# A graph layer on one core: one tile's rows picked by TensorE in 23 of 24 groups in place of 21

## The chip, the cores and the metric

One NeuronCore of a Trainium2 chip runs the kernel. The metric is device time in microseconds (us) of one execution. In the profile TensorE is PE (PEld its weight loads), VectorE DVE, ScalarE ACT, GpSimd POOL and SyncE SP.

## The reference

One layer of a graph network over 12,500 nodes with 64 features and 400,000 edges, sorted by destination, with 16 features each:

```python
m_in = concatenate([x[src], x[dst], edge_attr], axis=-1)
h = silu(m_in @ W1 + b1)
messages = silu(h @ W2 + b2)
agg = segment_sum(messages, dst, num_segments=12500)
node = silu(concatenate([x, agg], axis=-1) @ W3 + b3)
out = layernorm(x + node)
```

What matters here is `x[src]`: for every edge one row of `x` has to be fetched, in no order.

## The kernel before

**Tiles and groups.** Edges are taken in groups of 1024, as T = 8 tiles of 128 edges. There are 390 full groups and a short one of five tiles. Each tile is 128 rows of `edge_in`: a one-hot of the destination inside a window of 48 nodes (`OH`), the 64 features of the source node (`XS`) and the 16 of the edge (`EA`). `edge_in` has S = 12 slots, one a group. A body is B = 24 groups; there are 16 bodies and a rest. Every engine's order is written out by hand, as `step(g)` for g = 0 to 389.

**Gathers.** GpSimd issues one indirect DMA for each tile (`gather`, L508), eight to a group, with one index for each partition. From group 12 on, `refill` waits until TensorE has transposed the group that held the slot (`s_in_T`).

**Picks.** For some groups (`PICK_OF`) the last tile's rows (`PICKED` = 7) aren't gathered but picked by TensorE out of a copy of `x` that stays in SBUF (`parts`: two parts whose sum is x, 98 blocks of 128 nodes). GpSimd then issues seven gathers. A pick has two rounds (`ROUNDS`), as a PSUM bank holds 8 blocks of 64 features and there are 16 `PLACES`. It has NP = 13 pieces, seven in round 0 and six in round 1. A piece is two matmuls (`pick_piece`, L1086), one for each part, with the one-hot `rows_T` as weights and 512 columns moving; piece 6 holds two blocks only and moves 128 columns. So a pick is 24 matmuls of 512 and two of 128 columns. Three banks (`PICK_BANKS`) take the rounds in turn: the first piece of round number `at` waits until VectorE has read round `at - 3` (`s_picked`).

VectorE's part of a pick: `make_diag` (L827) and `make_rows` (L833, L836) build the keys and `rows_T` three and two groups ahead of the pick's first piece, with `find_rows` (L814 to L820) once for a chunk of eight groups; `pick` reads round 0 (L848), then round 1 (L852), and sums into `edge_in` (L854). TensorE spreads the keys in between (`spread_keys`, L1060).

**Which piece goes where.** `spot(piece)` gives the group in whose step TensorE runs a piece. `read_in` gives the group in whose step VectorE reads a round: the group of the round's last piece, or the one before when that piece is among the first `HALF_STEP` of its step.

```python
def spot(piece):
    return FIRST + piece * B // (PER_BODY * NP)
while spot(ended(PICKS, ROUNDS - 1)) + LEAD + 1 < FULL:
    PICKS += 1
TARGET = [spot(ended(n, ROUNDS - 1)) + LEAD + 1 for n in range(PICKS)]
HALF_STEP = PER_BODY * NP // (2 * B)
def read_in(n, r):
    e = ended(n, r)
    return spot(e) - (e < HALF_STEP or spot(e - HALF_STEP) < spot(e))
```

**TensorE's step(g)**: first layer of group g+1 (L1044, L1045); transposes of group g+2 (L1027), which wait for its gathers, its one-hots, and its picked rows if it has any; the pieces of g (L1086); a wait for the messages of g (`s_pair`, L801); second layer of g+1 (L1050), which waits for `h_T`; the key matmul, half of a lot's update (L1102) in two groups of a body, and the sums of group g (L1069).

**VectorE's step(g)**: bias of g+1 (L779, waits for L1050), window added (L807), one-hots of g+4 (L761 to L765), messages of g+1 paired (L790 to L801), `make_rows`, `make_diag`, `pick`, then a share of a lot.

**ScalarE's step(g)**: first silu of g+1 (L588), copy of the transposed g+2 (L584), edge features of g+4 (L579), second silu of g+1 (L592). In bodies 1 to 15 a lot of nodes that are complete is finished beside the groups: VectorE takes the mean in group 12 of the body, the squares in 13 and the variance in 14 (L884, L886). Behind the work of that step ScalarE waits for the variance, takes the root (L607) and loads the silu table again (L608), before it goes on with the first silu that TensorE's step of group 15 needs.

**SP** loads chunks of eight groups, and for each group a window of destination terms behind `s_z1`, and loads and stores the lots.

Of the kernel before, what the change touches and what calls it, by code (L numbers as in the profile page):

```python
# [23 lines left out]
def gnn_layer(nc, x, src, dst, edge_attr, W1, b1, W2, b2, W3, b3, out):  # L24
# [51 lines left out]

    PER_BODY = 21
    PICKED = T - 1  # L80
    PARTS = 2
    ROW_SETS, HOTS = 3, 4
# [15 lines left out]
    def spot(piece):  # L98
        return FIRST + piece * B // (PER_BODY * NP)

# [15 lines left out]
    KEYS_IN, ROWS_IN, DIAG_IN = ({b - back: n for n, b in enumerate(BEGUN)} for back in (2, 2, 3))  # L116
    HALF_STEP = PER_BODY * NP // (2 * B)

# [1075 lines left out]
```

## Time and profile before

| | |
|---|---|
| median of 3 runs | 3527.44 us (3524.67 to 3528.28) |
| the profiled execution | 3528.14 us |
| its span, first to last instruction | 3526.2 us |
| PE busy | 3265.4 us (93%), 18748 matmuls |
| PEld busy | 2500.9 us (71%) |
| DVE busy | 2965.4 us (84%) |
| ACT busy | 1052.2 us (30%) |
| POOL busy | 2642.7 us (75%), 2791 gathers |
| mean granted TensorE clock | 0.989 of full speed |

An engine's busy time is the union of its instructions' durations. Matmuls overlap, so the duration of one is longer than the time from its start to the next one's. Idle time is put down to what released the engine, "issue" where the profile shows nothing. All rows come from one profiled execution, whose start is 0.

### The profile page before, as it was taken

The page shows a single profiled execution, that of the slowest core. Times are in us where ns is not written, and L with a number is a line of the kernel's source. Part 1 is how long each engine was busy: PE and PEld are TensorE (multiplying, and loading weights), DVE is VectorE, ACT ScalarE, POOL GpSimd, SP SyncE. Part 2 cuts the span into 40 slices and gives each one's busy share as a digit, 9 for nine tenths or more (in the row PEclk, how much of TensorE's full clock was granted, in tenths as well). Part 3 has the DMA queues.
Part 4 walks back from the last instruction along what each step waited for, and adds up shares of the span by engine and source line. Part 5 has one row for each costly group of instructions (what it writes and reads, how often), then busy time and mean ns, then how long its engine had stood idle before and what let it go on. Part 6 is the DMA issues. An engine that isn't in the chain of part 4 may idle for free. (4 is left out here: it accounts for less than half of the span.)

```text
span 3526.2 us, 55961 instructions
## 1 busy us (share of the span) xinstructions
PE 3265.4 (93%) x18748; PEld 2500.9 (71%) x18748; DVE 2965.4 (84%) x6391; ACT 1052.2 (30%) x1687; POOL 2642.7 (75%) x2801
## 2 busy tenths in 40 slices
PE   4899999999999999999999999999999999999996
PEld 2677777777777777777777777777777777777774
DVE  7788888888888888888888888888888888888886
ACT  1322323323333233322323232232322323223232
POOL 7777777777777777777777777777777777777774
PEclk9899999999999999999999999999999999999998
DMA  7112221211222122122211212112121211222111
GB/s 176 36 36 42 40 42 35 49 36 37 40 42 42 36 45 39 37 40 42 42 35 38 46 35 42 36 38 46 38 40 36 49 35 38 40 42 42 34 31 28
DMA packets 324212, 150.08 MB, mean 43 GB/s; under 512 B 213310, under 2 KB 278879, under 8 KB 323926
## 3 DMA queue, kind: packets, MB, share of 16 engines
q0 software_dynamic: 89312, 91.63, 13.8%
q1 hardware_dynamic: 232774, 54.48, 7.4%
q8 instruction: 156, 2.56, 0.3%
q14 instruction: 130, 1.06, 0.1%
q10 hardware_dynamic: 1840, 0.34, 0.1%
HBM read 136.61 MB, written 9.62 MB: 41 GB/s over the span
## 5 line engine op out<-in xcount | busy, mean ns | idle before, releaser
L508 POOL DMA_INDIRECT edge_in<-in_x_dram,src_i x2791 | 2641.6, 946 | 852.1 <-issue 819.9
L1086 PE MATMUL pick_ps<-parts,rows_T 128*128 128x512 f32 (+1 forms) x8684 | 2052.7, 389 | 30.9 <-DVE kept L848 17.1
L1086 PEld LDWEIGHTS pick_ps<-parts,rows_T 128*128 128x128 f32 x8684 | 1554.4, 188 | 386.4 <-DVE kept L848 24.7
L592 ACT ACTIVATE z_ps<-z_ps,zero_col 128x512 f32<-128x512 f32 x391 | 258.8, 662 | 2107.1 <-DVE z_ps L779 2107.1
L1027 PEld LDWEIGHTS in_ps<-ident,edge_in 128*128 128x128 f32 x3128 | 339.4, 142 | 461.2 <-issue 314.6
L779 DVE TENSOR_TENSOR z_ps<-z_ps,b_rep 128x512 f32<-128x512 f32 x391 | 273.3, 699 | 395.7 <-PE z_ps L1050 395.1
L1027 PE MATMUL in_ps<-ident,edge_in 128*128 128x128 f32 x3128 | 427.5, 280 | 130.7 <-DMA edge_in<-in_x_dram,src_i 94.8
L1050 PEld LDWEIGHTS z_ps<-w_bd,h_T 128*128 128x128 f32 x3128 | 411.0, 194 | 70.1 <-issue 32.4
L584 ACT COPY in_T<-in_ps 128x1024 f32<-128x1024 f32 x391 | 396.9, 1015 | 194.1 <-PE in_ps L1027 189.5
L1050 PE MATMUL z_ps<-w_bd,h_T 128*128 128x128 f32 x3128 | 423.5, 279 | 33.7 <-ACT h_T L588 26.3
L1044 PE MATMUL z_ps<-in_T,w_in 128*64 128x512 f32 x782 | 411.8, 608 | 1.3 <-ACT in_T L584 1.2
L1045 PE MATMUL z_ps<-in_T,w_in 128*64 128x512 f32 x782 | 411.8, 608 | 0.0
L854 DVE TENSOR_REDUCE edge_in<-kept 128x64 f32<-128x512 f32 x334 | 355.5, 1064 | 11.5
L836 DVE TENSOR_TENSOR rows_T<-agg_ps,key_of 128x896 fp32r<-128x896 f32 x334 | 361.4, 1082 | 0.0
L794 DVE TENSOR_TENSOR z_ps<-z_ps,beyond 128x512 f32<-128x512 f32 x391 | 273.5, 699 | 13.5
L798 DVE TENSOR_REDUCE pair<-z_ps 128x64 f32<-128x512 f32 x391 | 270.3, 691 | 13.4
L588 ACT ACTIVATE h_T<-z_ps,b_col 128x512 f32<-128x512 f32 x391 | 266.5, 682 | 20.9 <-PE z_ps L1045 20.9
L790 DVE TENSOR_REDUCE every<-z_ps 128x64 f32<-128x512 f32 x391 | 266.0, 680 | 1.7 <-ACT z_ps L592 1.7
L852 DVE COPY_PREDICATED kept<-hot_place,pick_ps 128x512 f32<-128x512 int32 x334 | 244.1, 731 | 12.9
L848 DVE TENSOR_TENSOR kept<-pick_ps,hot_place 128x512 f32<-128x512 f32 x334 | 229.3, 687 | 15.2 <-DVE edge_in L854 0.5
L765 DVE TENSOR_TENSOR edge_in<-agg_ps,dst_rel 128x384 f32<-128x384 f32 x391 | 215.1, 550 | 0.0
L1069 PE MATMUL agg_ps<-edge_in,pair 128*64 128x48 f32 x1564 | 127.1, 242 | 4.0 <-DVE pair L801 4.0
(104 smaller groups left out, 1468.5 us busy)
## 6 DMA issues: line engine op xcount, KB each, us to landing
edge_in<-in_x_dram,src_i POOLq DMA_INDIRECT x2791
ea<-in_edge_attr_dram SPq DMA_DIRECT2D x48, 512.0 KB, 4.5
w_in<-node_terms SPq DMA_DIRECT2D x391, 12.0 KB
node_terms<-h_T SPq DMA_DIRECT2D x12, 256.0 KB, 2.4
node_terms<-lot_T SPq DMA_DIRECT2D x12, 256.0 KB, 2.4
y<-in_x_dram SPq DMA_DIRECT2D x15, 192.0 KB, 5.1
term<-node_terms SPq DMA_DIRECT2D x15, 192.0 KB, 5.0
out_dram<-y SPq DMA_DIRECT2D x15, 192.0 KB
```

The costliest lines, as they stand in the source:

```text
L508: pool.indirect_dma_start(out=edge_in[:, to_slot, t, XS], out_offset=None, in_=x[:, :], in_offset=bass.IndirectOffsetOnAxis(ap=indices[:, ...
L584: nc.scalar.copy(in_T[:, :, :], in_ps[:, :, :]).then_inc(s_in_c, 1)
L779: nc.vector.tensor_add(z2, z2, b2_rep[:, :].unsqueeze(1).to_broadcast([P, T, H])).then_inc(s_biased, 1)
L794: nc.vector.tensor_mul(messages, messages, beyond[:, v % 4, :].rearrange("p (a c) -> p c a", a=2).unsqueeze(3).to_broadcast([P, HT, 2, H]) ...
L798: nc.vector.tensor_reduce(pair[:, v % 2, 1, :], z2_ps[:, :].rearrange("p (k f) -> p f k", f=H), AX.X, ALU.add).then_inc(s_other, 1)
L836: nc.vector.tensor_tensor(rows_T[:, n % ROW_SETS, :, :], agg_ps[:, KEYS].unsqueeze(1).to_broadcast([P, SETS, P]), key_of[:, :].unsqueeze(2 ...
L854: nc.vector.tensor_reduce(edge_in[:, TARGET[n] % S, PICKED, XS], kept[:, :, :].rearrange("p k f -> p f k"), AX.X, ALU.add).then_inc(s_row, 1)
L1027: last = nc.tensor.transpose(in_ps[:, t // HT, t % HT * P:(t % HT + 1) * P], edge_in[:, s, t, :], ident[:, :])
L1044: nc.tensor.matmul(z1_ps[0:H, :], w_in[:, v % NW, :], in_T[:, 0, :], start=True, stop=True)
L1045: nc.tensor.matmul(z1_ps[H:P, :], w_in[:, v % NW, :], in_T[:, 1, :], start=True, stop=True).then_inc(s_z1, 1)
L1050: last = nc.tensor.matmul(z2_ps[:, c * P:(c + 1) * P], h_T[:, c * P:(c + 1) * P], w2_bd[:, :], start=True, stop=True)
L1086: last = nc.tensor.matmul(pick_ps[at % PICK_BANKS][:, 0:(b - a) * H], rows_T[:, n % ROW_SETS, c, :], parts[:, j, a:b, :].rearrange("p k f ...
```

## The change

One constant. In a body, 23 groups have their last tile picked in place of 21. Everything that is worked out from `PER_BODY` follows: how many picks there are (`PICKS`), where each piece stands (`spot`), which groups are picked (`TARGET`), when keys and rows are made, and when rounds are read (`HALF_STEP` goes from 5 to 6).

```diff
-    PER_BODY = 21
+    PER_BODY = 23
     PICKED = T - 1
     PARTS = 2
     ROW_SETS, HOTS = 3, 4
```

## Rows read from the trace of the kernel before

**Rows 1.** The chain that ended last, shares of the span by line.
```profile
POOL edge_in L508 17%; PE pick_ps L1086 4%; DMA edge_in<-in_x_dram,src_i 3%; PE in_ps L1027 2%; PE z_ps L1050 1%; PE z_ps L1044 0%; PE agg_ps L1102 0%; DVE z_ps L779 0%; PE agg_ps L1069 0%; PE pick_ps L1102 0%; DVE edge_in L765 0%; DVE beyond L764 0%; DVE sums L807 0%; DVE z_ps L794 0%; DVE every L790 0%
```

**Rows 2.** Groups of the whole span: shapes xcount | busy, mean ns | idle before, releasers.
```profile
L508 POOL DMA_INDIRECT edge_in<-in_x_dram,src_i x2791 | 2641.6, 946 | 852.1 <-issue 819.9 <-PE in_ps L1027 30.2 <-DMA src_i<-in_src_dram 2.0
L1086 PE MATMUL pick_ps<-parts,rows_T 128*128 128x512 f32 x8016 | 2034.3, 401 | 30.9 <-DVE kept L848 17.1 <-DVE kept L852 12.7
L1086 PEld LDWEIGHTS pick_ps<-parts,rows_T 128*128 128x128 f32 x8684 | 1554.4, 188 | 386.4 <-DVE kept L848 24.7 <-DVE rows_T L836 23.0 <-issue 15.2
...
L836 DVE TENSOR_TENSOR rows_T<-agg_ps,key_of 128x896 fp32r<-128x896 f32 x334 | 361.4, 1082 | 0.0
L854 DVE TENSOR_REDUCE edge_in<-kept 128x64 f32<-128x512 f32 x334 | 355.5, 1064 | 11.5
...
L852 DVE COPY_PREDICATED kept<-hot_place,pick_ps 128x512 f32<-128x512 int32 x334 | 244.1, 731 | 12.9
L848 DVE TENSOR_TENSOR kept<-pick_ps,hot_place 128x512 f32<-128x512 f32 x334 | 229.3, 687 | 15.2 <-DVE edge_in L854 0.5
...
L827 DVE TENSOR_SCALAR key_diag<-ident,find 128x128 fp32r<-128x128 f32 x334 | 96.3, 288 | 1.7
```

**Rows 3.** Who waited for whom, whole span: us in total, times, longest.
```profile
PE in_ps L1027 <- DMA edge_in<-in_x_dram,src_i: 94.8, 126, 4.1
```

**Rows 4.** Stretches: length, busy PE, PEld, DVE, ACT, POOL (instructions), PEclk, DMA share, GB/s.
```profile
120.80:423.30 302.50, 298.05 (x1732) 229.67 (x1733) 262.88 (x569) 90.42 (x146) 228.51 (x243) 1.00 0.21 40
423.30:631.00 207.70, 201.77 (x1159) 155.32 (x1161) 179.20 (x389) 63.59 (x102) 157.07 (x167) 0.98 0.21 40
837.40:1043.50 206.10, 199.49 (x1159) 153.28 (x1159) 179.35 (x389) 63.50 (x102) 155.84 (x166) 1.00 0.21 40
1886.70:2100.50 213.80, 200.25 (x1161) 153.25 (x1161) 179.64 (x389) 63.71 (x102) 161.71 (x172) 1.00 0.20 40
423.30:513.20 89.90, 85.44 (x478) 65.32 (x478) 74.54 (x162) 27.80 (x44) 68.05 (x72) 0.96 0.22 42
3470.50:3499.70 29.20, 18.44 (x102) 12.91 (x101) 16.93 (x36) 9.68 (x14) 19.07 (x21) 0.77 0.13 24
```

**Rows 5.** Timeline of PE, steps 7 and 11: start, us, what, count.
```profile
156.23 5.36 PE L1086 MATMUL pick_ps<-parts,rows_T 128*128 128x512 f32 x22
161.43 1.05 PE L1050 MATMUL z_ps<-w_bd,h_T 128*128 128x128 f32 x8
...
189.41 5.57 PE L1086 MATMUL pick_ps<-parts,rows_T 128*128 128x512 f32 x24
194.82 1.05 PE L1050 MATMUL z_ps<-w_bd,h_T 128*128 128x128 f32 x8
```

**Rows 6.** Timeline of PE and DVE, steps 4 and 8, around bank waits.
```profile
129.26 0.61 PE L1044 MATMUL z_ps<-in_T,w_in 128*64 128x512 f32 x1
...
131.08 3.67 PE L1086 MATMUL pick_ps<-parts,rows_T 128*128 128x512 f32 x16
...
134.55 0.68 DVE L848 TENSOR_TENSOR kept<-pick_ps,hot_place 128x512 f32<-128x512 f32 x1
...
135.29 1.65 PE L1086 MATMUL pick_ps<-parts,rows_T 128*128 128x512 f32 x6 [0.53 <-DVE kept L848]
...
162.63 0.61 PE L1044 MATMUL z_ps<-in_T,w_in 128*64 128x512 f32 x1
...
168.59 2.10 PE L1086 MATMUL pick_ps<-parts,rows_T 128*128 128x512 f32 x8 [0.42 <-DVE kept L852]
```

**Rows 7.** Timeline of DVE and PE, around group 15 of body 1.
```profile
431.16 0.17 DVE L886 TENSOR_SCALAR var<-var 128x6 f32<-128x6 f32 x1
...
433.90 2.04 PE L1050 MATMUL z_ps<-w_bd,h_T 128*128 128x128 f32 x8 [3.37 <-ACT h_T L588]
```

**Rows 8.** Timeline of PE, the last steps.
```profile
3494.69 0.67 PE L1044 MATMUL z_ps<-in_T,w_in 128*64 128x512 f32 x1
...
3499.68 0.61 PE L1044 MATMUL z_ps<-in_T,w_in 128*64 128x512 f32 x1
```

## The prediction, made before the change was built

> **What bounds the kernel now.** I read the chain that ended last first: the largest share it names is GpSimd's issue of gathers [rows 1]. The list of groups says why: 2791 gathers of 946 ns leave GpSimd idle for 852.1 us, of which 819.9 us is issue and 30.2 us a wait for TensorE [rows 2]. So it is always issuing, one gather each (2641.6 + 852.1) / 2791 = 1.25 us. TensorE waits 94.8 us for their landing [rows 3].
>
> The table of stretches then shows that this holds for only part of the run [rows 4]. A body is 24 groups and repeats itself. The stretch from the step of group 39 to that of group 63 (423.3 to 631.0 us) takes 207.7 us, the one two bodies later starting at 837.4 takes 206.1, while 171 gathers need 171 x 1.25 = 213.8 us: GpSimd, which began 12 groups ahead, is being caught up, and TensorE sets the pace, with 199.5 busy of 206.1 us. Five bodies on, one takes 213.8 us, GpSimd's pace. I take 206.3 for TensorE's own pace (near the lower of the two, as 207.7 holds a stretch of half clock), so it has only some 7.5 us to spare in a body, 0.3 us a group. This slack, not the 93% of the page, is what the change spends.
>
> **Gathers removed.** PICKS goes from 334 to 366 (the loop that sets it, counted), so 32 gathers go: a body has 23 x 7 + 8 = 169, or 211.3 us, and the whole floor of GpSimd falls by 40 us. That helps only where GpSimd is the bound.
>
> **Matmuls added.** Each pick is 26 matmuls, 24 of 512 columns and two of 128. The step of group 7 holds 22 long ones and no short: from 156.23 to the L1050 at 161.43 us, 0.236 us each. That of group 11, 22 long and two short, goes from 189.41 to 194.82 us, 5.41 against 5.20, so the short pair is 0.2 us [rows 5]. A pick costs 24 x 0.236 + 0.20 = 5.9 us, and two more in a body 11.8 us, its key matmul hidden in the rounding. They stand in TensorE's order ahead of the second layer, and nothing covers them once the 7.5 us are used: 206.3 + 11.8 = 218.1 us, already above 211.3. Bounds: the weight load alone, 0.188 us, below; 2034.3 / 8016 = 0.254 us, the busy time by count, above [rows 2]; 9.4 to 12.6 us a body. The 401 ns of one overlap and are no price. Even 9.4 leaves 215.7, above 211.3.
>
> By LDWEIGHTS the same bodies look far less full: 153.3 of 206.1 us, 74% [rows 4]. The Trainium skill, Perfetto Trace Analysis, Identifying the Most-Contended Engine, calls matmul busy time a bad measure of the distance to roofline and puts LDWEIGHTS busy % in its place. By that rule a quarter of TensorE would be free and the 12 us would fit: it is the first rival below. I go by the pace, since 24 groups took 206 us while GpSimd's gathers were ahead.
>
> **The wait for banks.** There are three PSUM banks, so a round waits until VectorE has read the round three before. I place each wait by hand. Pick k of a body begins 13k/24 pieces into its step (before: 1.625k), so offsets now creep: 0 0 1 1 2 2 3 3 ... 11, where they jumped 0 1 3 4 6 8 9. VectorE reads a bank at a fixed point: in the step that starts at 129.26 its L848 runs 134.55 to 135.23 and TensorE resumes at 135.29, 6.0 us into the step [rows 6]. At offset 1 TensorE has seven long pieces of 0.47 us and a short one of 0.2 behind its start at 131.08, and stands there 5.3 us into the step; each piece of offset moves that by 0.47 us. That is a wait of 1.2 us at offset 0, 0.7 at 1, 0.25 at 2, none from 3. For picks 1 to 5 of a body: 1.2 + 0.7 + 0.7 + 0.25 + 1.05 = 3.9 us (pick 5 meets find_rows, 0.8 us ahead of the reads in that VectorE step). The first round of a pick waits too, for the second round of two picks before, once that one is read a group later (from pick 12 on): in the step at 162.63 TensorE reached offset 8 and lost 0.6 us until L852 was done [rows 6]. Now five picks (14 to 18) meet this, at offsets 7, 8, 8, 9, 9, each with some 0.2 of key_diag's 288 ns ahead of the read: 1.3 + 0.8 + 0.8 + 0.3 + 0.3 = 3.5 us. Sum 7.4 us, against 3 x (0.74 + 0.6) = 4.1 us now: +3.3 us a body. Bounds: nothing, and twice this.
>
> **The wait for ScalarE at group 15 of a body.** ScalarE holds the next silu back until the lot's variance is there, then loads a table. In TensorE's pace: variance (L886) at 431.16, L1050 at 433.90 after 3.37 us idle [rows 7]. Today that VectorE step holds only L848 ahead of the variance. With offsets of the new rule both reads and the L854 sum stand there: + 0.16 + 0.77 + 1.0 = 1.9 us. Against it VectorE is less late from the steps before, whose TensorE steps are a piece longer (two of them with lot work, each 0.47 us longer: about 1 us less late, an estimate), and the matmuls ahead of the wait end 0.47 us later: net +0.5 us. Bounds 0 and +2. A half clock followed such waits: 0.96 in the 89.9 us from 423.3, 1.00 in the body from 837.4 [rows 4]; its cost is inside the 206.3.
>
> **VectorE and the rest.** 32 picks more are 32 x (1082 + 1064 + 731 + 687 + 288 ns) = 123 us of VectorE [rows 2]. In a body it was busy 179.4 of 206.1 us [rows 4]; with 7.7 us more in 221.9 it has more air, and I price it at nothing beyond the waits above. ScalarE issues nothing new. SP's chunks, windows and lots are unchanged in number and wait for L1045, so they slide with TensorE; no DMA is added. GpSimd will wait for TensorE to free slots, which costs nothing.
>
> **Sum.** A body: 206.3 + 11.8 + 3.3 + 0.5 = 221.9 us, TensorE's pace all through. The step of group 3 starts at 120.8 us, that of group 39 302.5 us later [rows 4]; these 1.5 bodies gain 1.5 x 15.1 = 22.6, so 445.9. Fourteen bodies: +3106.6 = 3552.5 (group 375). The last ten groups with pieces took 89.9 us in TensorE's pace [rows 4]; with 10/24 of 11.8, 1.2 of bank waits and 0.5: 96.5, so 3649.0. Four steps with no pieces, 3499.68 - 3494.69 = 5.0 us each [rows 8], give 3669; now they wait for gathers and take 29.2 us [rows 4]. The last 26.5 us (3499.7 to the end at 3526.2) stay. Span 3695.5; around it lie 1.9 us (3528.1 against 3526.2), so 3697 us. The profiled execution is 0.7 us above the median of the runs, less than I can price.
>
> **Rivals.** (1) The other sign: GpSimd stays the bound, because TensorE's 26% without weight loads is usable; the time is 3528 - 40 = 3488 us. The point that decides is a TensorE body below 211.3 us, where the measured one plus bare matmuls is 218.1. (It is what the page of the Trainium skill named above would have.) For it: TensorE's largest wait is for gathers [rows 3]. Against: rows 4. 4%.
> (2) The waits do not grow: a body of 217.9 to 218.1, hence 1.5 x 3.3 + 14 x 3.8 + 1.7 = 60 us less, 3637 us. The later bodies show waits that vanish when TensorE starts late. But in TensorE's pace nothing makes it late. 10%.
> (3) The waits compound: the wait at group 15 grows by 2 us and each is followed by the half clock, as at 423.3 (207.7 against 206.1, another 1.6 us, of which 0.2 is in my 206.3). Each of 15 bodies costs up to 3 us more and some 2.5 in the mean: 3735 us. 12%.
> (4) Gathers and matmuls trade evenly: 211.3 against 211 or so, about 3527. It needs matmuls at half price. 2%.
> That the change does not do what it says I rule out by the count of PICKS.
>
> **Numbers.** My forecast has 72%, rivals 2 and 3 are its flanks, so the range runs 3630 to 3740. A measurement here tells 0.2% (7 us) from no change. Faster: rival 1, 4%. Within 0.2%: 2%. Slower: 94%.
>
> **What would show it.** Matmuls at L1086 9516, gathers 2759. GpSimd's wait for L1027 hundreds of us instead of 30.2; TensorE's wait for gathers near nothing. Bodies near 222 us from the second on. L1086's idle time before it grown from 30.9 us [rows 2] to some 80 to 110; L1050's wait for h_T near 4 us in every body. Wrong would be bodies at 211 us, or a GpSimd that still never waits, or waits at offsets other than those listed.

## The result, and the profile after

The changed kernel takes **3722.94 us** (median of four runs, 3720.05 to 3725.03), against 3527.86 us (3524.67 to 3530.31, four runs) for the kernel before. The ratio is 1.0552, 95% interval 1.0538 to 1.0565: slower by 5.5%, 195 us. Forecast was 3697 us in a range of 3630 to 3740.

The page of the changed kernel, its span and its busy times:

```profile
span 3723.2 us, 58073 instructions
PE 3482.3 (94%) x19612; PEld 2671.5 (72%) x19612; DVE 3088.6 (83%) x6615; ACT 1052.4 (28%) x1687; POOL 2611.4 (70%) x2769
```

TensorE is busy 217 us longer than the 3265.4 before, at nearly the same share; VectorE 3088.6 - 2965.4 = 123.2 us longer. GpSimd is busy 31 us less, and that helps nobody: the chain that ended last, which began with 17% of gathers [rows 1], now holds no line of GpSimd, though it is short and reaches back only to 3585.8 us, so the groups and stretches below have to carry the reading. The groups of the whole span, shapes and count, then busy time and mean ns, then idle time before them and its releasers:

```profile
L508 POOL DMA_INDIRECT edge_in<-in_x_dram,src_i x2759 | 2610.2, 946 | 991.7 <-issue 852.5 <-PE in_ps L1027 137.2 <-DMA src_i<-in_src_dram 2.0
L1086 PE MATMUL pick_ps<-parts,rows_T 128*128 128x512 f32 x8784 | 2228.4, 401 | 94.0 <-DVE kept L848 47.7 <-DVE kept L852 45.2
L1027 PE MATMUL in_ps<-ident,edge_in 128*128 128x128 f32 x3128 | 436.2, 283 | 11.4 <-DVE edge_in L765 11.4
L1050 PE MATMUL z_ps<-w_bd,h_T 128*128 128x128 f32 x3128 | 429.6, 282 | 73.6 <-ACT h_T L588 57.6 <-DVE pair L801 16.0
```

Against [rows 2]: 32 gathers fewer, and 768 long matmuls more. The transposes (L1027) wait no more for a gather, where they lost 94.8 us [rows 3]; GpSimd waits for the transposes instead, 137.2 us against 30.2. The idle time before the pick matmuls went from 30.9 to 94.0 us, and VectorE's two reads of banks (L848, L852) share it. Each group says where to look next: who is late has changed from GpSimd to TensorE.

The table of stretches, in the columns of [rows 4]: the steps of groups 3 to 37, then a body each in the second, fourth and tenth place.

```profile
120.80:439.50 318.70, 309.14 (x1767) 238.64 (x1769) 268.89 (x575) 88.04 (x142) 240.94 (x256) 1.00 0.17 37
447.40:671.60 224.20, 214.51 (x1213) 164.76 (x1211) 186.93 (x403) 63.65 (x102) 169.65 (x180) 0.98 0.18 39
895.90:1119.20 223.30, 213.38 (x1212) 163.85 (x1211) 187.02 (x402) 63.69 (x102) 163.95 (x174) 0.99 0.18 38
2237.90:2460.80 222.90, 213.33 (x1210) 164.21 (x1209) 186.61 (x402) 63.70 (x102) 159.14 (x169) 0.99 0.18 38
```

Before, an early body took 206.1 to 207.7 us and a late one 213.8, when GpSimd had been caught up. Now early and late are alike at 223 to 224: one engine sets the pace from one end to the other, and its busy time is 213.3 to 214.5 us of it. GpSimd needs 169 x 1.25 = 211.3 us a body, some 12 us less. The weight loads fill 164 of 223 us, 73%, the same share as before. That is the number by which TensorE looked a quarter free, and yet a body with two picks more takes 17 us longer.

### The profile page after: what moved, and what is told of

It is laid out like the page before. It is cut to its first block and busy times, and to the rows that moved or that the text cites. A ratio compares the mean times of both kernels' runs of the same rounds, so it can differ in the third digit from the quotient of the medians.

```text
span 3723.2 us, 58073 instructions
## 1 busy us (share of the span) xinstructions
PE 3482.3 (94%) x19612; PEld 2671.5 (72%) x19612; DVE 3088.6 (83%) x6615; ACT 1052.4 (28%) x1687; POOL 2611.4 (70%) x2769
## 5 line engine op out<-in xcount | busy, mean ns | idle before, releaser
L508 POOL DMA_INDIRECT edge_in<-in_x_dram,src_i x2759 | 2610.2, 946 | 991.7 <-issue 852.5
L1086 PE MATMUL pick_ps<-parts,rows_T 128*128 128x512 f32 (+1 forms) x9516 | 2255.3, 390 | 94.0 <-DVE kept L848 47.7
L1086 PEld LDWEIGHTS pick_ps<-parts,rows_T 128*128 128x128 f32 x9516 | 1703.1, 188 | 494.2 <-DVE kept L848 59.9
L1027 PEld LDWEIGHTS in_ps<-ident,edge_in 128*128 128x128 f32 x3128 | 342.6, 143 | 341.1 <-issue 308.3
L1050 PEld LDWEIGHTS z_ps<-w_bd,h_T 128*128 128x128 f32 x3128 | 419.5, 197 | 113.4 <-issue 63.6
L1050 PE MATMUL z_ps<-w_bd,h_T 128*128 128x128 f32 x3128 | 429.6, 282 | 73.6 <-ACT h_T L588 57.6
L1027 PE MATMUL in_ps<-ident,edge_in 128*128 128x128 f32 x3128 | 436.2, 283 | 11.4 <-DVE edge_in L765 11.4
L1044 PE MATMUL z_ps<-in_T,w_in 128*64 128x512 f32 x782 | 419.9, 619 | 1.4 <-ACT in_T L584 1.4
L1045 PE MATMUL z_ps<-in_T,w_in 128*64 128x512 f32 x782 | 419.9, 619 | 0.0
L854 DVE TENSOR_REDUCE edge_in<-kept 128x64 f32<-128x512 f32 x366 | 389.4, 1064 | 12.6
L836 DVE TENSOR_TENSOR rows_T<-agg_ps,key_of 128x896 fp32r<-128x896 f32 x366 | 396.3, 1083 | 0.0
L852 DVE COPY_PREDICATED kept<-hot_place,pick_ps 128x512 f32<-128x512 int32 x366 | 267.5, 731 | 17.3
L848 DVE TENSOR_TENSOR kept<-pick_ps,hot_place 128x512 f32<-128x512 f32 x366 | 251.5, 687 | 16.8 <-DVE edge_in L854 0.5
```

Source lines behind the costliest of these rows:

```text
L508: pool.indirect_dma_start(out=edge_in[:, to_slot, t, XS], out_offset=None, in_=x[:, :], in_offset=bass.IndirectOffsetOnAxis(ap=indices[:, ...
L836: nc.vector.tensor_tensor(rows_T[:, n % ROW_SETS, :, :], agg_ps[:, KEYS].unsqueeze(1).to_broadcast([P, SETS, P]), key_of[:, :].unsqueeze(2 ...
L854: nc.vector.tensor_reduce(edge_in[:, TARGET[n] % S, PICKED, XS], kept[:, :, :].rearrange("p k f -> p f k"), AX.X, ALU.add).then_inc(s_row, 1)
L1027: last = nc.tensor.transpose(in_ps[:, t // HT, t % HT * P:(t % HT + 1) * P], edge_in[:, s, t, :], ident[:, :])
L1044: nc.tensor.matmul(z1_ps[0:H, :], w_in[:, v % NW, :], in_T[:, 0, :], start=True, stop=True)
L1045: nc.tensor.matmul(z1_ps[H:P, :], w_in[:, v % NW, :], in_T[:, 1, :], start=True, stop=True).then_inc(s_z1, 1)
```

## The experiments

Two theories stood about where the 195 us lie. **Theory P (pace and waits):** TensorE's order with its waits is the bound, so a body costs its matmuls, the bank waits, the wait for h_T, and a half clock after that wait. Then what shortens the waits gives time back. **Rival M (the matmuls alone):** the added matmuls cost what they cost, and the waits are only room that TensorE has anyway. A second rival, from the other side (rival 1 of the prediction), was that weight loads or gathers bound the kernel and bare matmuls are nearly free.

One thing has to be known for the ratios: in all experiments but `p22`, the chip took 4458 to 4512 us for the kernel before, where it took 3528 us when the change was timed. So each figure is set against the kernel before as timed beside it, and the first run to look at is the changed kernel itself there. In the code shown, `...` marks what is left out.

**a_again, the changed kernel once more.** 

> The changed kernel itself, as a reference on a chip of this call, since the chips of the two calls before took 4466 and 4512 us for the kernel before. Where the kernel before takes 3528 us: 3723 us, ratio 1.055. Where it takes some 4500 us: theory, TensorE's pace sets the time there too and is stretched by stalls of its own, so 832 more matmuls and the longer waits cost at least their 200 us: ratio 1.04 to 1.06. Rival: the stalls there cover the waits for banks and for h_T, and only the matmuls' 190 us are left, of which some overlap: ratio 1.01 to 1.03.

Measured: 4541.84 us against 4457.81, ratio 1.0192 (1.0163 to 1.0221). That lies in the range of the rival, not of the theory. The change is slower here too, by 84 us instead of 195. The groups of its whole span:

```profile
L508 POOL DMA_INDIRECT edge_in<-in_x_dram,src_i x2759 | 2610.6, 946 | 1799.9 <-issue 892.1 <-PE in_ps L1027 561.8 <-remote 344.0
L1086 PE MATMUL pick_ps<-parts,rows_T 128*128 128x512 f32 x8784 | 2363.6, 417 | 387.3 <-DVE kept L848 164.4 <-DVE kept L852 131.5 <-issue 79.1
L1027 PE MATMUL in_ps<-ident,edge_in 128*128 128x128 f32 x3128 | 479.6, 291 | 124.3 <-issue 111.8 <-DVE edge_in L765 11.2
L1050 PE MATMUL z_ps<-w_bd,h_T 128*128 128x128 f32 x3128 | 456.9, 294 | 89.0 <-ACT h_T L588 53.2 <-issue 20.8 <-DVE pair L801 15.0
L1060 PE MATMUL agg_ps<-key_diag,ones_r 128*128 128x128 f32 x366 | 117.2, 320 | 1.3 <-issue 1.1 <-DVE key_diag L827 0.2
```

The same program, instruction for instruction, and the gathers are as long as before (946 ns). What grew most is idle time. TensorE's is 782 us (span less busy time) instead of 241; 387 us of it stand before the pick matmuls instead of 94, 296 of them put down to VectorE's reads. TensorE's busy time grew as well, from 3482.3 to 3750.5 us, at a mean granted clock of 0.922 instead of 0.983. The waits before L1086 are here the largest item of TensorE's idle time. So this condition of the chip is a poor place to ask for the price of a matmul.

The clocks bear on the 84 us too. Beside this run the kernel before ran at 0.892 and the changed one at 0.921, in the mean of their runs. Time at half speed costs at most (1 - 0.892) x 4458 = 481 us in the first and (1 - 0.921) x 4542 = 359 us in the second. These 122 us are about what the change costs less here than in the other condition (195 - 84 = 111 us). No run separates the two, so this stays an estimate.

**p22, PER_BODY = 22,** half of the change, and the one kernel measured where the kernel before took 3528 us.

```diff
-    PER_BODY = 21
+    PER_BODY = 22
```

> PER_BODY 22, nothing else changed. Where the kernel before takes some 3528 us: a body of TensorE is 206.3 + 5.9 = 212.2 us plus or minus some us of waits (picks begin at offsets 0, 1, 2 ... 11, so the waits are 0.7 and 0.25 us at the second round, 1.3, 0.8 and 0.3 at the first, in each half body: 6.7 us against 4.1), or 214.8 us, against 212.5 us for 170 gathers. Theory: TensorE sets the pace, total 3570 to 3600 us, ratio 1.012 to 1.02, so the loss grows faster than the matmuls from 21 to 23. Rival (GpSimd stays the bound): 3508 us, ratio 0.994. Where the kernel before takes some 4500 us: between 1 and the 1.019 of 23 of 24.

Measured: 3605.10 us (3603.72 to 3606.8) against 3528.56, ratio 1.0217 (1.0200 to 1.0234), 5 us above the upper end of what was expected. Its groups, and two of its bodies:

```profile
L1086 PE MATMUL pick_ps<-parts,rows_T 128*128 128x512 f32 x8400 | 2133.4, 401 | 74.6 <-DVE kept L852 56.8 <-DVE kept L848 15.4
L1050 PE MATMUL z_ps<-w_bd,h_T 128*128 128x128 f32 x3128 | 429.2, 281 | 73.1 <-ACT h_T L588 58.3 <-DVE pair L801 13.3 <-issue 1.5
```

```profile
426.90:643.10 216.20, 208.19 (x1184) 159.64 (x1183) 183.16 (x396) 63.69 (x102) 163.53 (x173) 0.98 0.21 40
1507.90:1724.90 217.00, 208.37 (x1184) 159.94 (x1183) 182.76 (x396) 63.69 (x102) 163.98 (x175) 0.98 0.21 39
```

With 21, 22 and 23 picks a body, TensorE's pace is 206.3, 216.4 and 223.75 us (for 22 and 23 the mean of fourteen bodies from group 39 on): the first pick more costs 10.1 us, the second 7.4. One pick's matmuls are 5.9, so 4.2 us of the first step are something else. The groups name it. Idle time before L1086 is 4.6 us a body in the mean of those fourteen, where the bodies of before from 631.0, 837.4 and 1043.5 us, in TensorE's pace, show 2.5, 3.4 and 2.5. L1050 waits for h_T 3.80 us in the body of group 63, and 58.3 / 15 = 3.9 in the mean, where those three show 3.2. That is some 1.8 + 0.7; the rest is of the size of what the half clock and the restarts after a wait cost, which comes last below. With 23 picks the h_T wait is no longer (57.6 us) and only the bank waits grow on (94.0). A body of 216.4 is above the 212.5 us that GpSimd needs with 170 gathers, so the kernel with 22 is bound by TensorE as well: one pick more is enough for that.

**e4 and f4, the matmuls alone.** The kernel before with 21 picks, the first matmul of each round issued twice: 668 more matmuls of 512 columns, all gathers and all reads as they were.

```diff
                 done_with = (r, c + 1) not in PIECES
+                if c == 0:
+                    nc.tensor.matmul(pick_ps[at % PICK_BANKS][:, 0:(b - a) * H], rows_T[:, n % ROW_SETS, c, :],
+                                     parts[:, 0, a:b, :].rearrange("p k f -> p (k f)"), start=True, stop=True)
                 for j in range(PARTS):
```

> The kernel before (21 of 24), with the first matmul of each round run twice: 42 more matmuls of 512 columns in a body, 668 in all, no gather removed and nothing for VectorE. Theory (TensorE has 7.5 us to spare in a body, and each costs 0.236 us): a body is 206.3 + 9.9 = 216.2 us against GpSimd's 213.7, and the time 3590 to 3610 us. Rival A (by weight loads a quarter of TensorE is free): 3528 us, no change. Rival B (the slack was larger, as GpSimd's pace covers the waits): a body of 213.7, and under 3545 us.

> The kernel before (21 of 24), with the first matmul of each round run twice: 668 more matmuls, 42 in a body, no gather removed and nothing for VectorE. On a chip where the kernel before takes 3528 us. Theory (7.5 us to spare in a body, 0.236 us each): a body 206.3 + 9.9 = 216.2 us or less, as the added matmul stands ahead of a wait for a bank only in part, time 3575 to 3610 us. Rival A (by weight loads a quarter of TensorE is free): 3528 us. On the slow chip the same kernel came out within 0.2% of the kernel before.

Measured: ratio 1.0017 (1.0004 to 1.0030), and again 1.0011 (1.0000 to 1.0021), that is 5 and 2 us between the medians for what would be 668 x 0.236 = 158 us if it were exposed. Rival A's number came, and the theory's didn't. Two groups of the second one, L1086 being the matmuls added:

```profile
L508 POOL DMA_INDIRECT edge_in<-in_x_dram,src_i x2791 | 2638.4, 945 | 1706.6 <-issue 753.7 <-PE in_ps L1027 495.4 <-remote 455.5
L1086 PE MATMUL pick_ps<-parts,rows_T 128*128 128x512 f32 x668 | 307.2, 460 | 106.5 <-DVE kept L848 49.8 <-issue 28.8 <-DVE kept L852 26.3
```

GpSimd waits 495 us for TensorE's transposes, so gathers alone are not the bound here; and yet the matmuls cost next to nothing. Two things can pay for them, and there is no profile of the kernel before in this condition to weigh them. TensorE still stands idle for 684 of 4460.6 us, so added work can lie in that room. And the granted clock is 0.908 where the kernel before has 0.892 beside it, which is worth (1 - 0.892) x 4467 - (1 - 0.908) x 4469 = 71 us at most. In either case the price of a matmul is not one number: 0.236 us where TensorE's order is packed (206.3 to 223.75 us a body), next to nothing here. It does not test the price in the 3528-us condition, for which it was meant; there the steps of the trace have to do.

**e1 and f1, the banks read first.** VectorE's step reads the pick's banks ahead of building the next rows and keys, so that TensorE's bank waits (theory P) end earlier; everything else as in the changed kernel.

```diff
+                for n, r in READ_IN.get(g, ()):
+                    pick(n, r)
                 if g in ROWS_IN:
                     make_rows(...)
                 if g in DIAG_IN:
                     make_diag(...)
-                for n, r in READ_IN.get(g, ()):
-                    pick(n, r)
```

> The changed kernel (23 of 24), with VectorE reading the rounds (L848, L852, L854) ahead of make_rows and make_diag in its step, so that each bank comes free 1.35 us sooner. Theory (TensorE sets the pace, and waits for banks some 7 us in a body): L1086's idle time falls from 94.0 us to under 15, a body from 223.7 to some 216.5 us, and the time from 3723 to about 3615 us. Rival A (the added matmuls alone make the time, and the waits for banks are covered by other work): within 10 us of 3723. Rival B (VectorE's added work of 123 us makes it): no change either, as its work is the same.

> The changed kernel with the rounds read ahead of make_rows and make_diag, on a chip where it takes 3723 us. Theory (the waits for banks are on TensorE's path, 7 us in a body): L1086's idle time from 94 to under 15 us, a body from 223.7 to some 216.5 us, time about 3615 us. Rival A (the added matmuls alone make the loss): within 10 us of 3723. New since the slow chip's trace: the key matmul L1060 may wait for L836, which the edit makes later; by the rows it is ready 0.5 us ahead of need, so under 20 us in all.

Measured: 1.0076 (1.0059 to 1.0092) and 1.0080 (1.0062 to 1.0098) of the kernel before, against 1.0192 for the change. The edit gives back 1.1% of the 1.9%, where 2.9% was expected (across two chips; for the same kernel, `e3_both` and `r3_both` below, two chips differ by 0.3%). The groups of f1 show the trade:

```profile
L1086 PE MATMUL pick_ps<-parts,rows_T 128*128 128x512 f32 x8784 | 2314.8, 412 | 144.9 <-DVE kept L848 54.2 <-issue 52.4 <-DVE kept L852 37.1
L1050 PE MATMUL z_ps<-w_bd,h_T 128*128 128x128 f32 x3128 | 430.9, 282 | 115.7 <-ACT h_T L588 98.2 <-DVE pair L801 10.4 <-issue 7.0
L1060 PE MATMUL agg_ps<-key_diag,ones_r 128*128 128x128 f32 x366 | 115.4, 315 | 251.1 <-issue 131.4 <-DVE rows_T L836 68.1 <-DVE key_diag L827 50.3
```

The idle time before L1086 falls from 387 to 145 us, where under 15 was expected. But 250 us appear before L1060, TensorE's key matmul, whose key VectorE now makes last (68 us for L836 alone, expected under 20), and the wait for h_T grows from 53 to 98. TensorE's idle time as a whole is 779 us against 782 in a_again: the waits have moved, and none of the 242 us is left as idle time won. The profiled execution is 28 us shorter because TensorE is busy 26 us less. So by this edit alone theory P is not shown.

**e2 and f2, the root a group later.** ScalarE takes the lot's root, and loads its table, one group later, so that the variance is there when ScalarE comes to it. VectorE's normalising (`LOT_NORM`) moves a group later with it.

```diff
-    LOT_READ, LOT_SUM, LOT_SILU, LOT_MEAN, LOT_SQ, LOT_STD, LOT_NORM, LOT_STORE = 8, (9, 10), 11, 12, 13, 14, 15, 17
+    LOT_READ, LOT_SUM, LOT_SILU, LOT_MEAN, LOT_SQ, LOT_STD, LOT_NORM, LOT_STORE = 8, (9, 10), 11, 12, 13, 15, 16, 17
```

> The changed kernel, with ScalarE's root and table load one group later (LOT_STD 15, LOT_NORM 16). ScalarE then finds the variance ready. Theory: the 15 waits of L1050 for h_T (57.6 us) go, and with them most of the half clock that follows each, worth 1 to 2 us a time: 3723 falls by 75 to 90 us to about 3640 us, and the mean clock rises above 0.99. Rival A (such a wait would be made up for later, as other engines catch up in it): under 15 us less. Rival B (only the wait goes, and the clock's share is nothing): 58 us less, 3665 us.

> The changed kernel with ScalarE's root one group later, on a chip where it takes 3723 us. Theory: the 15 waits for h_T (57.6 us) and most of the half clock behind them go: 3640 us, mean clock above 0.99. Rival A (made up for by waits elsewhere): over 3705 us. Rival B (the clock's share is nothing): 3665 us.

Measured: 1.0088 (1.0067 to 1.0109) and 1.0099 (1.0083 to 1.0116). The groups of f2:

```profile
L1086 PE MATMUL pick_ps<-parts,rows_T 128*128 128x512 f32 x8784 | 2383.3, 420 | 434.0 <-DVE kept L852 164.2 <-DVE kept L848 155.1 <-issue 99.8
L1050 PE MATMUL z_ps<-w_bd,h_T 128*128 128x128 f32 x3128 | 449.1, 290 | 23.0 <-ACT h_T L588 10.8 <-DVE pair L801 8.7 <-issue 3.5
```

The wait for h_T falls from 53.2 to 10.8 us, the idle time before L1050 from 89 to 23, and the kernel is about 1.0% faster than the change, some 45 us where 75 to 90 was expected. The idle time before L1086 stays, and grows a little (387 to 434), so TensorE's idle time as a whole falls by 14 us only, to 767 (26 us in e2). The mean granted clock is 0.923, against 0.922, so the expected rise of the clock did not come here.

**e3, r3 and f3, both edits.**

> The changed kernel with both: rounds read first, root one group later. Theory: a body's TensorE work alone is about 210 us, just below the 211.3 us that GpSimd needs for 169 gathers. GpSimd becomes the bound again, and the time is about 3495 us, below both kernels. Rival A (TensorE stays the bound because the waits were covered by nothing but replaced by others): above 3540 us. Rival B (the two parts are independent and additive to the last): 3723 - 108 - 85 = 3530 us.

> The changed kernel with both edits (rounds read ahead of make_rows and make_diag; root one group later), again, since the chip of the first four runs took 4466 us for the kernel before, against 3528 us. Where the kernel before takes some 3528 us: theory, TensorE's own work is about 210 us in a body, just below the 211.3 us of 169 gathers, so GpSimd is the bound again and the time about 3495 us. Rival A: above 3540 us, because other waits take the place of those removed. Rival B, plain addition: 3723 - 108 - 85 = 3530 us. Where the kernel before takes 4466 us again: the ratio stays at 0.993.

> The changed kernel with both edits, on a chip where it takes 3723 us and the kernel before 3528. Theory: TensorE's own work, some 210 us in a body, is just below the 211.3 us of 169 gathers, so GpSimd is the bound again: 3490 to 3505 us, below both kernels. Rival A (the waits come back at another place, L1060 for L836 above all): above 3540 us. Rival B (plain addition): 3723 - 108 - 85 = 3530 us.

Measured: 0.9928 (0.9911 to 0.9944), on another chip 0.9955 (0.9937 to 0.9973), and again 0.9924 (0.9908 to 0.9941). With both edits the 23 picks are *faster* than the kernel before by 0.45 to 0.76%, in the condition where they alone are 1.9% slower. From 1.0192 to 0.9926 is 2.7%, 119 us. e1, e2 and e3 were timed together on one chip, and so were f1, f2 and f3. There the second edit added to the first gives 1.5 to 1.6% (e1 to e3, f1 to f3), and the first added to the second 1.6 to 1.8% (e2 to e3, f2 to f3). That is more than either gave against a_again (1.1 and 1.0%), though the 0.3% between chips leaves the size of this surplus open. The groups of the last one:

```profile
L1086 PE MATMUL pick_ps<-parts,rows_T 128*128 128x512 f32 x8784 | 2323.9, 413 | 140.0 <-issue 60.9 <-DVE kept L848 45.0 <-DVE kept L852 32.2
L1050 PE MATMUL z_ps<-w_bd,h_T 128*128 128x128 f32 x3128 | 421.5, 278 | 22.8 <-DVE pair L801 10.2 <-ACT h_T L588 9.8 <-issue 2.8
L1060 PE MATMUL agg_ps<-key_diag,ones_r 128*128 128x128 f32 x366 | 113.4, 310 | 268.8 <-issue 118.9 <-DVE key_diag L827 89.9 <-DVE rows_T L836 59.2
```

Both waits are small at once here: 140 us before L1086 and 22.8 before L1050, where either edit alone left one of the two and, with f1, made the h_T wait longer (98.2 us). That the second edit takes this growth away again fits their giving more together. TensorE's idle time as a whole is now 708 us, 74 less than in a_again, and its busy time 23 less, which is the 96 us by which the profiled execution is shorter. Rival M, that the waits are room which costs nothing, does not fit this: not one matmul fewer, and 2.7% less time. One part of the expectation failed: GpSimd is not the bound, since it still waits 449 us for TensorE's transposes. What these edits are worth where the kernel before takes 3528 us wasn't measured. By the terms measured below at most 8.1 us of bank waits and 3.8 + 2.5 us for h_T and what follows it could go in a body, about 200 us in 14 bodies; how much of it moves to L1060, as in f1, stays open, and so does the sign against the kernel before.

**a_fewer_gathers,** the changed kernel with 14 gathers taken out (2745 in its trace; the expectation counted 15).

```diff
-        return TT if g == FULL else T - picked(g)
+        return TT if g == FULL else T - (picked(g) or g >= 3 * S)
```

> The changed kernel, from group 36 on with seven gathers in every group: in the groups that aren't picked (15 of them, one in each body) the last tile isn't gathered, and takes what lies in its slot. It leaves that part of the input out. TensorE, VectorE and ScalarE do the same work. Theory (TensorE sets the pace, GpSimd waits for it): within 5 us of the changed kernel in the same call. Rival (GpSimd is still the bound in the later bodies): 15 x 1.25 = 19 us less.

Measured: 4487.39 us, 1.0057 (1.0039 to 1.0074), so 54 us less than the change in a_again, timed together with it. Neither theory had that: the gathers would be some 18 us if GpSimd were the bound, and nothing if it weren't. Waits for TensorE before GpSimd's gathers went from 561.8 to 631.1 us, so GpSimd did get more air. In the trace 50 us of the gain stand before L1086, whose idle time is 336.9 us instead of 387.3; why VectorE's reads come sooner there I couldn't settle. It is a miss, and left open. It also sets a measure for the edits above: a change that has nothing to do with banks or the root moved this kernel by 1.2% in this condition, so a single 1% does not prove its cause, and the argument rests on the 2.7% of both edits.

## Why the prediction was right, and where it was off

**The bound moved, as said.** The point of decision was a TensorE body below or above 211.3 us. It is 223.75. Rival 1, in which the quarter of TensorE without weight loads takes up the matmuls, fell by it. The Trainium skill's page Perfetto Trace Analysis (Identifying the Most-Contended Engine) puts two numbers in place of matmul busy time, the share of peak FLOP/s (MFU) and the weight loads' busy share; the prediction took the second alone. That one disagrees with the trace for this kernel, since it stayed at 73 to 74% while TensorE went from nearly the bound to the bound. The first was not worked out here. In e4 and f4 added matmuls were nearly free, as rival 1 has it, but TensorE had 684 us of idle time there; the share of the weight loads (63%) doesn't say how much of that can be used.

**Counts and VectorE.** 9516 pick matmuls and 2759 gathers, as forecast; VectorE 123.2 us longer, forecast 123. That it cost nothing beyond the waits fits the bodies: 187 of 223 us.

**The matmuls.** TensorE's busy time in a body rose from 199.5 (at clock 1.00, [rows 4]) to 213.4 us (at 0.99), by 13.9. The forecast had 11.8 for the matmuls; the half clock, under which every instruction is longer, and the restarts after waits are in the rest. Steps without a wait agree with the price of a piece: they take 7.97 us with 20 long and two short matmuls, and 8.44 with 22 long and two short, so (8.44 - 7.97) / 2 = 0.235 us each, forecast 0.236. Summed over the 24 steps of a body, each at the length that it has without a wait, TensorE's work is 197.5 us before and 209.4 after: 11.9 us more.

**The bank waits stand where they were put.** The forecast named picks 1 to 5 and 14 to 18 and the point at which TensorE resumes, 6.0 us into the step. Timeline of the changed kernel, the pick that begins in group 76, the first of those with a wait after group 75, as start, duration, what, and idle before it:

```profile
795.40 0.61 PE L1044 MATMUL z_ps<-in_T,w_in 128*64 128x512 f32 x1
...
797.22 3.20 PE L1086 MATMUL pick_ps<-parts,rows_T 128*128 128x512 f32 x14
...
800.69 0.68 DVE L848 TENSOR_TENSOR kept<-pick_ps,hot_place 128x512 f32<-128x512 f32 x1
...
801.42 2.60 PE L1086 MATMUL pick_ps<-parts,rows_T 128*128 128x512 f32 x10 [1.00 <-DVE kept L848]
...
805.06 0.61 PE L1044 MATMUL z_ps<-in_T,w_in 128*64 128x512 f32 x1
```

TensorE runs 14 matmuls, seven pieces, from 797.22, is done at about 800.4, stands until VectorE has read the bank (800.69 + 0.68) and resumes at 801.42, 6.02 us into the step that began at 795.40. The step takes 805.06 - 795.40 = 9.66 us where the same work without a wait takes 8.44: 1.22 us lost, forecast 1.2. Taken so for each of them, against steps that wait for nothing, the five picks at the front of the body lose 1.22 + 0.77 + 0.76 + 0.30 + 1.04 = 4.1 us (forecast 3.9), the five behind 1.33 + 0.84 + 0.85 + 0.40 + 0.45 = 3.9 (forecast 3.5). So 8.0 us in this body (groups 63 to 86) for 7.4, and 8.1 in the mean of fourteen. What the forecast took for today was a little off by itself: its 3 x (0.74 + 0.6) is 4.0, not 4.1.

**The wait at group 15** was to go from 3.37 us by +0.5. Timeline of the step of group 63 of the changed kernel:

```profile
680.55 0.17 DVE L886 TENSOR_SCALAR var<-var 128x6 f32<-128x6 f32 x1
...
683.29 2.05 PE L1050 MATMUL z_ps<-w_bd,h_T 128*128 128x128 f32 x8 [3.91 <-ACT h_T L588]
...
685.62 1.08 PE L1044 MATMUL z_ps<-in_T,w_in 128*64 128x512 f32 x1
...
689.11 6.28 PE L1086 MATMUL pick_ps<-parts,rows_T 128*128 128x128 f32 x26
...
696.42 0.61 PE L1044 MATMUL z_ps<-in_T,w_in 128*64 128x512 f32 x1
```

3.91 us for 3.87. It comes back in each of the 15 bodies, a mean of 57.6 / 15 = 3.8 us, where before it was long in the early bodies alone (26.3 us in 15): the "near 4 us in every body" of the forecast.

**The term that was mis-sized is the half clock.** L1050 takes 2.05 us after the wait, L1044 1.08 us where it takes 0.61 us ten us later, and the stretch of these two steps says the same in its granted clock:

```profile
671.72:696.42 24.70, 20.79 (x104) 15.69 (x104) 15.93 (x42) 7.97 (x12) 18.61 (x21) 0.86 0.17 36
```

A granted clock of 0.86 in 24.70 us is 6.9 us at the lower level, 1.2 instead of 2.4 GHz, and at half speed these cost 3.5 us at most. The two steps take 13.90 and 10.80 us; with 8.69 (24 long matmuls and no short one) + 3.91 and 8.90 of work and wait, 3.2 us are left. The same two steps of other bodies, before from 837.4 and 1043.5, after from 896.0:

```profile
837.37:858.07 20.70, 17.07 (x99) 12.65 (x99) 15.82 (x37) 7.88 (x12) 15.83 (x17) 1.00 0.14 29
1043.53:1065.19 21.66, 18.45 (x99) 13.51 (x99) 15.98 (x37) 7.97 (x12) 16.48 (x18) 0.92 0.16 29
896.01:919.22 23.21, 19.41 (x105) 14.32 (x104) 15.83 (x41) 7.97 (x12) 17.69 (x19) 0.93 0.17 37
```

Before, from 837.4, the clock did not fall at all (1.00), and 0.2 us are left besides wait and work (11.67, with 8.22 of work and 3.21 of wait): that much a stop costs beyond its idle time, as at the bank wait above, 1.22 us lost for 1.00 idle. From 1043.5 (0.92, some 3.4 us at the lower level) 1.8 us are left, and as much from 631.0. After, from 896.0 (0.93) it is 1.8 us again. In the fourteen bodies after, these two steps show 0.86 eight times and 0.93 six times, so a mean of 5.4 us at the lower level, and never 1.00.

The forecast called this cost "inside the 206.3", with 0.2 us of it there, and let it grow by nothing. It took 206.3 us for the body of 206.1 and 0.2 us of half clock. But the body from 837.4 lost 5.2 us at bank waits, while those from 631.0 and 1043.5 lost 3.7 and 3.8 and had 1.6 us of half clock each: nearly the same length, made up otherwise. Term by term, us in a body, the mean of the three bodies from 631.0, 837.4 and 1043.5 before and of the fourteen from group 39 on after (rounded, so columns add up to within 0.1):

| | before | after | growth | forecast |
|---|---|---|---|---|
| work of the 24 steps | 197.5 | 209.4 | 11.9 | 11.8 |
| lost at bank waits | 4.2 | 8.1 | 3.9 | 3.3 |
| idle for h_T | 3.2 | 3.8 | 0.6 | 0.5 |
| what else the two steps lose, the half clock above all | 1.3 | 2.5 | 1.2 | 0 |
| body | 206.3 | 223.75 | 17.5 | 15.6 |

So the steps of the sum that were mis-sized are the half clock, 1.2 us for nothing, and after it the growth of the bank waits, 3.9 for 3.3. I priced the wait and not what follows it, though rival 3 named that term. Over fourteen bodies the difference is 14 x 1.85 = 26 us, of 28 by which the profiled execution (3725.0 us) lies above 3697. The two ends fit: the step of group 39 began at 447.6 us (forecast 445.9), and from group 375 to the end there were 143.2 us (143.0).

**One expected sign did not come** in its size: GpSimd's wait for L1027 is 137.2 us, not "hundreds". GpSimd is ahead by the twelve slots it has, so what it could wait is bounded by the gap between its last gather and the end. The lines of its gathers, number, min/median/max in ns, first and last start, of the changed kernel:

```profile
L508 POOL DMA_INDIRECT edge_in<-in_x_dram,src_i x2759: 938/944/1997, 4.0 to 3602.9; - x198
```

The last gather starts 120 us before the end, against some 30 before: the missing idle time stands behind the last gather, where the list of waits doesn't count it. I had forgotten this tail.

**The rivals.** Rival 2 (waits don't grow, 3637) fell with the 8.0 us; rival 3 (3735) named the right term and took too much for it, as the wait grew by 0.6 us and not by 2; rival 4 fell by the bodies.

## What to carry to other kernels

When two engines run close, compare their paces from a stretch in which each one is the bound (an early stretch, before the one ahead is caught up), not from busy shares or weight loads; the slack is the difference, here 7.5 of 206 us, and a change that hands work over spends it at once. Price a wait of TensorE with what follows: an idle time of 3.2 to 3.9 us was followed by another 0.2 us where the clock stayed, and by 1.8 to 3.2 us where it fell to half. And waits of a loop can be worth more than the work added, but judge an edit of them by the engine's whole idle time, since a wait taken away at one place can come back at the next, as in f1: with the reads put first and the root a group later, 23 picks went from 1.9% above the kernel before to 0.7% below it, in the condition in which that was measured.

## What was unexpected of the hardware

The same kernel, the one before, took 3528 us at some times and 4458 to 4512 us at others, on one chip both (the chip of `p22` also gave 4466 and 4467 for the kernel before). Little of the extra time is in instruction lengths: gathers took 946 ns in both, and TensorE, at a granted clock of 0.922 instead of 0.983, was busy 268 us longer. The larger part, 541 us on TensorE, is idle time, which the trace partly puts down to "remote" and "issue", on all engines. The waits of the changed kernel in a_again, in total, times, longest, us:

```profile
DVE z_ps L779 <- remote: 352.7, 48, 11.9
ACT h_T L588 <- remote: 311.6, 157, 5.7
POOL edge_in L508 <- remote: 344.0, 145, 4.1
```

None of these three is in the list of waits where the same kernel took 3723 us. On TensorE single transposes stand apart instead of running as a train of eight, timeline of the same run:

```profile
1704.66 0.27 PE L1027 MATMUL in_ps<-ident,edge_in 128*128 128x128 f32 x1 [0.83 <-issue]
1706.07 0.37 PE L1027 MATMUL in_ps<-ident,edge_in 128*128 128x128 f32 x1 [1.14 <-issue]
1707.48 0.47 PE L1027 MATMUL in_ps<-ident,edge_in 128*128 128x128 f32 x1 [1.03 <-issue]
```

They had waited for nothing that the profile names. What holds the engines up I can't say from these traces; I only see that idle time grew more than the work itself, and that waits are a larger part of the kernel: there two edits of the order were worth 2.7% together, and 668 matmuls 0.1 to 0.2%. Which is why a ratio from one condition is not carried to the other without saying so.
